# Four blocks on one core: the layer loop written out, the first weights in three parts, the experts' steps in a new order

## What is computed

```
x = x + layernorm(mamba(layernorm(x)))        # projections, 4-tap convolution, selective scan over 16 states
x = x + layernorm(tree(layernorm(x)))         # soft decision tree, 8 levels, 256 leaves
x = x + layernorm(retention(layernorm(x)))    # 4 layers: 8-head retention with decay, then a gelu ffn
x = x + layernorm(experts(layernorm(x)))      # 8 experts, each 128 -> 128 -> 128 with gelu; argmax of the gate chooses one
```

## Time and profile before

| | |
|---|---|
| median of 3 runs | 801.12 us (799.25 to 803.32) |
| the profiled execution | 800.74 us, its span (first to last instruction) 798.6 us |
| PE busy | 665.1 us, 83% of the span |
| DVE busy | 622.3 us, 78% |
| POOL busy | 429.0 us, 54% |
| ACT busy | 420.3 us, 53% |
| DMA | 27.38 MB, nearly all in the first 21 us and during the scan |

### The profile page before, as it was taken

How to read it: one execution, slowest core, us unless ns; L and a number is a source line. 1 busy time by engine, 2 the same in 40 slices (tenths; PEclk the granted TensorE clock), 3 DMA queues, 4 the chain that set the end, 5 groups by cost and what they waited for, 6 DMA issues and landing times. The chain is left out here.

```text
span 798.6 us, 13603 instructions
## 1 busy us (share of the span) xinstructions
PE 665.1 (83%) x4791; PEld 434.2 (54%) x4800; DVE 622.3 (78%) x1519; ACT 420.3 (53%) x731; POOL 429.0 (54%) x380
## 2 busy tenths in 40 slices
PE   2997798898988834757799997999979999788985
PEld 1444444444534333635576765667756676656764
DVE  4479898999989695556788887788858887778876
ACT  1896786786767316445554443444434444354641
POOL 6113588686877757564555555355535555551312
PEclk9998899999999976869999999999999999989998
DMA  8001133233343100000000000000000000000000
GB/s 318 5 5 53 40 93 97 77 91 79 89 96 80 53 2 0 0 1 2 2 1 22 2 6 15 21 2 5 14 3 21 2 14 5 2 1 1 15 14 27
DMA packets 17008, 27.38 MB, mean 34 GB/s; under 512 B 2288, under 2 KB 7024, under 8 KB 16560
## 3 DMA queue, kind: packets, MB, share of 16 engines
q1 hardware_dynamic: 16944, 26.51, 11.8%
HBM read 25.32 MB, written 1.18 MB: 33 GB/s over the span
## 5 line engine op out<-in xcount | busy, mean ns | idle before, releaser
L585 POOL TENSOR_TENSOR arena<-arena 128x1024 f32<-128x1024 f32 x64 | 150.0, 2361 | 54.5 <-PE psum L1343 35.1
L1008 DVE TENSOR_TENSOR_SCAN arena<-arena,psum 128x1024 f32<-128x1024 f32 x64 | 142.0, 2269 | 3.8 <-issue 2.0
L525 POOL TENSOR_TENSOR ve<-mv,eps 128x4 f32<-128x4 f32 x52 | 15.9, 306 | 218.3 <-DVE mv L909 218.3
L1343 PE MATMUL psum<-arena,Cs 128*128 128x512 f32 x256 | 124.2, 608 | 1.2 <-POOL arena L585 1.2
L723 ACT ACTIVATE arena<-arena 128x510 f32<-128x510 f32 x128 | 84.9, 711 | 54.0 <-DVE arena L1008 52.0
L632 POOL TENSOR_TENSOR arena<-arena,mhalf 128x32 f32<-128x32 f32 x16 | 86.9, 5428 | 2.3 <-DVE arena L1125 2.3
L1430 PE MATMUL psum<-arena,Wl 128*128 128x512 f32 x128 | 67.5, 640 | 8.5 <-DVE arena L1109 5.3
L1235 PE MATMUL psum<-Cs,arena 128*128 128x128 f32 x240 | 39.6, 290 | 41.9 <-ACT arena L766 25.8
L1343 PEld LDWEIGHTS psum<-arena,Cs 128*128 128x128 f32 x256 | 45.7, 193 | 47.0 <-issue 35.4
L1235 PEld LDWEIGHTS psum<-Cs,arena 128*128 128x128 f32 x240 | 29.0, 148 | 60.0 <-ACT arena L766 27.0
L1242 PEld LDWEIGHTS psum<-Wl,arena 128*128 128x128 f32 x384 | 47.1, 194 | 16.1 <-DVE arena L1134 9.4
(11 more groups left out here) (172 smaller groups left out, 1422.0 us busy)
## 6 DMA issues: line engine op xcount, KB each, us to landing
arena<-c_rows_by_state SPq DMA_DIRECT2D x32, 512.0 KB, 4.8
Wl<-wl SPq DMA_DIRECT2D x4, 384.0 KB, 3.1
Wa<-wa SPq DMA_DIRECT2D x1, 1251.0 KB, 7.1
Wd<-wd SPq DMA_DIRECT2D x1, 1100.0 KB, 12.3
X<-x SPq DMA_DIRECT2D x4, 256.0 KB, 7.7
Sel<-sel SPq DMA_DIRECT2D x1, 1024.0 KB, 9.6
Wl<-wl SPq DMA_DIRECT2D x4, 256.0 KB, 2.6
out<-X SPq DMA_DIRECT2D x4, 256.0 KB, 2.3
```

What stands on the lines that cost most here:

```text
L585: pool.tensor_tensor(Hc[:, h], Hs[:, r, h], Crows[:, r], ALU.mult).then_inc(hc_ready, 1)
L1008: dve.tensor_tensor_scan(Hs[:, turn % 2, h], Da[:, h], rows_of(turn, h), 0.0, ALU.mult, ALU.add).then_inc(scanned, 1)
L1343: ins = pe.matmul(bank[h], ident, Hc[:, h, group(e)], start=False, stop=False, skip_group_check=True)
```

## The change

Three things change. **The loop** over the later layers is no hardware loop any more: each engine's program holds the three turns of `LAYER` one behind the other, and all counts are constants. **The start**: `Wa` is loaded in three transfers with a semaphore each (the columns for the first products, the convolution's taps, the rest); DVE forms group 0's statistics before it waits for any weight and normalises group 0 before it turns to group 1, POOL takes group 0's power before the taps' products and the others' before `DiagD`, and ACT's exponential of `alog` goes behind the first copy of turned rows. **The experts**: the numbers in `EXPERT_SCHEDULE` change, and with them the order of `ENDING` on all engines. `SCHEDULE`, `LAYER` and `OPENING` stay as they were.

```diff
 EXPERT_SCHEDULE = (
-    (4.336, "r_stats", 0), (4.723, "r_norm", 0), (4.959, "x_stats", 0), (5.016, "x_norm", 0), (5.195, "d_turn", 0),
...
+    (4.235, "r_stats", 0), (4.450, "r_norm", 0), (4.728, "x_stats", 0), (4.893, "x_norm", 0), (5.065, "d_turn", 0),
...
+            wa_parts = ((slice(WA["x"].start, WA["dtw"].stop), wa_in), (WA["tap"], tap_in),
+                        (slice(WA["out"].start, WA["ln_b"].stop), wa_rest_in))
...
-                    sync.dma_start(Wa[:], wa).then_inc(wa_in, 16)
+                    for cols, landed in wa_parts:
+                        sync.dma_start(Wa[:, cols], wa[:, cols]).then_inc(landed, 16)
...
+            rstd(0)
             pool.wait_ge(wa_in, 16)
+            pool.wait_ge(tap_in, 16)
             for k in range(TAPS):
...
+            for g in range(1, G):
+                rstd(g)
             pool.wait_ge(ident_in, 16)
+            pool.wait_ge(wa_rest_in, 16)
...
-            for g in range(G):
-                rstd(g)
...
-            dve.wait_ge(wa_in, 16)
+            dve.wait_ge(x_in[0], 16)
+            stats(X3, 0)
             dve.wait_ge(dt_w, 1)
             dve.tensor_copy(Wdt, bank[7][:, 0:256]).then_inc(dt_wc, 1)
-            for g in range(G + 1):
+            normalise(Xn3, X3, 0, a_normed)
+            dve.wait_ge(wa_rest_in, 16)
+            for g in range(1, G + 1):
                 if g < G:
                     dve.wait_ge(x_in[g], 16)
                     stats(X3, g)
-                if g >= 1:
+                if g >= 2:
                     normalise(Xn3, X3, g - 1, a_normed)
...
-            with pe.Fori(0, LAYERS - 1) as layer:
-
-                before, first = last_fills(LAYER, layer, -1), last_fills(OPENING, layer, 0)
-                for b in before:
-                    held[b] = [before[b]] + ([first[b]] if b in first and first[b][1:] != before[b][1:] else [])
+            for layer in range(LAYERS - 1):
                 layer_steps(LAYER, layer)
```

More of the change, by code:

```diff
@@ L124, in __init__ @@
     def __init__(self, eng, sem):
-        self.eng, self.sem, self.n, self.turns = eng, sem, 0, None
+        self.eng, self.sem, self.n = eng, sem, 0
     def put(self, ins):
@@ L131, in settle @@
     def settle(self):
[L132 to L140, removed]
+        self.eng.wait_ge(self.sem, self.n)
 class Counter:
     def __init__(self):
-        self.n, self.turns = 0, None
+        self.n = 0
     def next(self):
         self.n += 1
[L151 to L159, removed]
+        return self.n
 class PerGroup:
@@ L172, in at @@
         turn, ahead = layer
[L173 to L177, removed]
+        count = (turn + ahead + self.primed) * self.per * G + self.per * g + (self.per if k is None else k)
+        assert count > 0
+        return self.sem, count
 SCHEDULE = (
@@ L637, in _ @@
                     layer_steps([step], 0)
-            with pool.Fori(0, LAYERS - 1) as layer:
-                own.enter(layer, PER_LAYER_POOL)
-                norms.enter(layer, 3 * G)
+            for layer in range(LAYERS - 1):
                 layer_steps(LAYER, layer)
-                own.leave(LAYERS - 1)
-                norms.leave(LAYERS - 1)
             for step in ENDING:
@@ L661, in _ @@
             own = Steps(act, act_steps)
-            act.wait_ge(wa_in, 16)
-            own.put(act.activation(Aneg, Wa[:, WA["alog"]], ACT.Exp))
-            own.settle()
-            act.mul(Aneg, Aneg, -1.0).then_inc(a_neg, 1)
             act.wait_ge(pads, 2)
@@ L674, in _ @@
             input_rows(0)
+            act.wait_ge(wa_rest_in, 16)
+            own.put(act.activation(Aneg, Wa[:, WA["alog"]], ACT.Exp))
+            own.settle()
+            act.mul(Aneg, Aneg, -1.0).then_inc(a_neg, 1)
             for g in range(G):
@@ L860, in _ @@
             act.preload_act_table(ACT.Gelu_apprx_tanh)
-            with act.Fori(0, LAYERS - 1) as layer:
-                own.enter(layer, PER_LAYER_SCALAR)
+            for layer in range(LAYERS - 1):
                 layer_steps(LAYER, layer)
-                own.leave(LAYERS - 1)
             one = (0, 0)
@@ L1151, in _ @@
                     layer_steps([step], 0)
-            with dve.Fori(0, LAYERS - 1) as layer:
+            for layer in range(LAYERS - 1):
                 assert not due
-                own.enter(layer, PER_LAYER_VECTOR)
-                norms.enter(layer, 3 * G)
                 layer_steps(LAYER, layer)
-                own.leave(LAYERS - 1)
-                norms.leave(LAYERS - 1)
             assert not due
@@ L1411, in claim @@
                 return bank[b]
-            def last_fills(order, turn, shift):
-                return {b: (reader, (turn, ahead + shift), g, k) for what, _, g, ahead in order for b, reader, k in FILLS.get(what, ())}
             def layer_steps(order, turn):
```

19 lines of the change are left out of this document (9 added, 10 removed).

## The result

The changed kernel takes 780.31 us (median of 4 runs, 779.56 to 781.24) beside 801.98 for the kernel before in its 4 runs; the ratio is 0.9735 (95% interval 0.9705 to 0.9764). That is 21.7 us by the medians. The profiled executions took 781.24 and 800.74, 19.5 apart, and the comparison of the traces explains these 19.5: the start 2.45, the scan 2.16, the layers 10.49, the experts' stage 3.97 by the traces' marks, the rest (0.4) lies outside the spans and in the stretches between. The marks that cut the two traces are the scan's first fill (PE's first product of the scan), DVE's first and last scan, the `heads` of the layers and the last instruction.

A forecast was written before the change was run, and what follows sets the result against it. PE was taken as the bound in the layers. From 800.74 us the loop (10.3), the start (4.4) and the experts (3.3) were subtracted, giving 782.7 us; forecast 780 to 785 at 0.48, wider range 775 to 790.

The forecast's parts named there:

- Loop, 10.3 us: Layers: removing PE's two jumps saves 4.88 and 5.46 us, together 10.3; other engines' jumps and register steps count nothing.
- (d): Loop: PE's 3.3 us are a fetch written-out code needs too; loop gives 0, time 793.0; chance 0.03.
- (e): Written-out turns: fetches fall behind, about 5 us per late block on PE, 813 with two per turn; chance 0.03.
- Start, 4.4 us: Start: earlier normalisation and split weights bring the scan forward 4.4 us; 3.2 with a late landing, 6.3 by PE's advance.
- rival (c): Start: split load costs what early normalisation wins, `x` of group 1 lands near 14; time 786.6; chance 0.09.
- PE's first turn near 9.2: Start: group 0's normalised rows let PE make its first turn near 9.2 us, 6.3 us earlier.
- Experts, 3.3 us: `ENDING`: the new order fills PE's waits for a gain of 3.3 us, from -1 to 5.9.
- The second wait: `ENDING`: PE's 2.88 us wait ahead of `out` of group 2; three moved PE steps fill 2.2 us of it.
- the third with its follower: `ENDING`: PE's 1.20 us wait ahead of `out` of group 3 and what it drags behind; gain 0 to 2.2, taken 1.1.
- the first wait: `ENDING`: PE's 2.79 us wait ahead of `ffn_turn` of group 1; DVE's `r_norm` ahead of it counted as 0.7 loss.
- Rival (a): Experts: the new order wins nothing, DVE's extra steps cost what PE gains; time 787; chance 0.20.
- (b): Experts: the order wins more, 6 to 9 us, no half clock and fewer waits; 777 to 780; chance 0.17.

The follow-up runs named there:

- PE's loop alone: The kernel before with the loop written out on PE only, the other engines keeping the hardware loop: 790.71 us, ratio 0.9855.
- the exponential first: The changed kernel with ACT's exponential of `alog`, and with it the table load, ahead of the first copy again: 779.24 us, ratio 0.9717.
- the taps held back: The changed kernel with POOL's products of the taps made to wait until DVE has normalised group 0: 780.46 us, ratio 0.9729.
- one transfer: The changed kernel with the first weights in one transfer and one semaphore: 781.76 us, ratio 0.9747.
- the two kernels on the last steps: The changed kernel with `t_norm` back at 7.172: 781.74 us; with it at 7.950 and ACT's table loaded at its very start: 781.22 us.

## Why the prediction was right, and where it was not

**Loop, 10.3 us: right.** The two traces give 10.49, PE's loop alone 10.8 by the medians of its runs (801.47 - 790.71). The reading that carried it was the branch row beside the stretches. Its steps held one by one: in the layers the other engines' jumps and the registers cost nothing, and written-out code ran without a stall. The price of a jump varies a little: 4.88 and 5.46 in the earlier trace rows, 4.85 and 4.88 in the kernel where PE alone loops. Rivals (d) and (e) are out. The 108 ns that the Trainium skill gives (Advanced Engine Details and Errata, Control Flow Timing) are a thirtieth of what PE's jump takes; DVE's 63 and ACT's 45 ns lie below them.

**Start, 4.4 us: the right sign, too much.** The pair of profiles gives 2.45, the means of four executions each 3.35. In these eight the fill stands 51.8 to 52.2 us behind L949 (L966 before), so what sets L949 sets the gain. One profile is no measure of this term: the landing of the weights differs by 1.3 us between executions of the same start (5.80 to 7.06), and L1247 (L1268 before), for which L949 waits through ACT, took anything from 1.05 to 1.92 us. The transfers came out as the sum had them: the first part landed at 6.47 (6 taken) and `x` of group 1 at 9.42 (9.8 taken), so rival (c) is out. The fixed time per transfer of the Trainium skill (SBUF — State Buffer, section on the DMA setup-cost knee) did not add up here: the three parts were all landed at 8.52, where the one transfer had landed at 8.84.

What failed is the step "PE's first turn near 9.2", and with it the estimate that ACT is done by 17 ahead of L949: the turn came at 10.88, and ACT's L661 ended at 20.71. L949 was to gain what PE gains, 6.3 us, or 4.5 where DVE's row bounds it; it gained 2.5, since three terms were missing on the way through PE and ACT. DVE's normalised rows were priced at 1.11 from the earlier trace rows, where POOL had done its products before; beside them they take 1.9 to 2.9, and with a landing 0.5 later than taken the turn is 1.7 late. The edit that moves ACT's exponential behind the first copy moves the table load too, which had been out of the way (1.3); I gave that edit no price at all. And L1247 still runs at the slow pace of PE's first products, in which L1246's four take 3.78 us that take 1.88 from group 1 on, where before L1268 no longer did (0.9). 6.3 - 1.7 - 1.3 - 0.9 = 2.4. The diff and the order show the first two: what is taken off one engine's front stands somewhere else, and what ran beside it changes.

The clash has a page that I didn't use. The Trainium skill (SBUF — State Buffer, Who interferes with whom) says that DVE and GpSimd share a pair of ports to SBUF (the memory that the engines work on), taken for a whole instruction, and names `tensor_scalar` among those that can take it, and DVE instructions with two inputs in SBUF beside a GpSimd one that reads SBUF. The traces agree: 1.11 alone, 2.62 beside the taps, 2.05 beside the sum. They do not agree for POOL's power, which slows no such instruction (last section).

**Experts, 3.3 us: the right mechanism, somewhat too little.** The traces give 3.97: 4.3 of idle time, 0.9 of clock, 1.2 lost in the tail. The second wait fell from 2.88 to 0.35 (2.2 taken), the third with its follower from 2.2 to nothing (1.1 taken), the clock gave 0.9 (1.2 taken), the tail cost 1.24 (1.1 taken), the first wait went from 2.79 to 2.93 (0.1 in all was taken). The forecast that the waits for L1218 stay was wrong (2.6 to 1.4). Not foreseen were the two waits for ACT's L834, 2.1 us: right behind `ffn_up` PE now has `d_turn`, which fills the same PSUM bank (1 in `FILLS`) and so waits for ACT's gelu of that `ffn_up`, and ACT loads a table first, since it comes from the gelu of a `hidden`, which is another function (`Gelu`, not `Gelu_apprx_tanh`). Before, a `hidden` and an `expert` stood there.

```profile
700.94 1.28 ACT L834 ACT_TABLE_LOAD   x1
702.23 1.09 ACT L834 ACTIVATE arena<-psum 128x512 f32<-128x512 f32 x2
```

Against the kernel with the old order the stage gains 5.0 us by the profiles (125.09 to 120.10) and 6.5 by the medians. More executions narrow this. Five have the old order in the last stage and five the unaltered new one (the changed kernel twice, the exponential first, the taps held back, one transfer): 124.59 us on average against 119.72, a gain of 4.9. Idle time of PE gives 4.1 of it (12.2 to 12.7 us in each of the old, 8.3 to 8.4 in each of the new), busy time 1.85, and the tail costs 1.05. The busy time is the clock's: 6.8 to 10.2 us at half clock with the old order, 0 to 6.8 with the new. Taken were 3.2 of idle time (-0.7 + 0.6 + 2.2 + 1.1) and 1.2 of the clock, so both were set too low, and the clock's part differs between executions of one order. Rival (a) is out; only the medians reach into (b). That the tail's price is real and yet could not be had back by moving the step alone, the two kernels on the last steps show.

**The sum.** 18.0 us were forecast and 782.7 us; measured are 21.7 by the medians and 780.31 us, inside the range. The second measurement of the changed kernel gives 19.5 (801.17 - 781.7). By the means the parts are loop 10.5, start 3.4 and experts 4.9, together 18.8; the rest is the scan's clock and the medians' own spread (the kernel before ran from 798.63 to 805.16 us over all its runs here). That the sum came so close is in part luck: the start was set 1.0 us too high and the experts 1.6 too low.

## What to carry to other kernels

Read a loop's price from the stretch that holds its jump, on the engine that bounds it: here two jumps of PE cost 10 us of 800 and those of the four other engines nothing that shows in the layers. When work moves forward on one engine, look at what now runs beside it on the others (here POOL's products beside DVE's rows), and at the table load that was hidden by the instruction moved away. Measure a term of 2 or 3 us on marks inside the trace, counted from the transfer that starts it, and on more than one execution.

## What the runs showed of the hardware

DVE and POOL met in more places than the start, and there they held each other up. In the layers of the changed kernel DVE's product L1113, with both operands in SBUF, begins as POOL's L615, a sum of the same size, does (min/median/max ns over all their executions):

```profile
L1113 DVE TENSOR_TENSOR arena<-arena x16: 681/1752/1757, 386.9 to 703.6; 128x512 f32<-128x512 f32 x16
L615 POOL TENSOR_TENSOR arena<-arena x32: 1266/1277/1729, 353.8 to 656.6; 128x512 f32<-128x512 f32 x32
```

Without L615 beside it, L1113 takes 681 ns; in the 13 of 16 groups where they meet it takes 1.75 us, and the second of the two L615 there 1.72 instead of 1.27. It costs nothing there, since PE bounds the group. POOL's power L620 (5.43 us, 128x32) does not do this: all 60 of DVE's L900 that ran wholly beside it took at most 344 ns (343 in the middle without POOL). DVE's instructions with an operand in PSUM that I compared were not slowed by POOL (the scans L991 took 2.26 to 2.29 us beside POOL's L573 and 2.26 to 2.28 alone; PSUM is the memory of PE's products). The second surprise is the jump: 3.3 to 3.9 us on PE and 0.04 to 0.07 on the other four engines, for branches of the same kind over turns of different length.
